# Cross-attention by head halves: another order of the steps on four engines

## What is computed

```
q = einsum('bld,hed->bhle', layernorm(x), Wq) + bq      # 8 heads of 128
k, v = the same from the context
scores = einsum over a window of 64 keys, spaced by (1,1,2,2,4,4,8,8)[head]
out = softmax(scores) @ v_win
x = x + out.reshape(..., 1024) @ Wc.T + bc
```

## Time and profile before

| | us |
|---|---|
| median of 3 runs | 492.98 (492.39 to 494.41) |
| the profiled execution | 493.77 |
| its span, first to last instruction | 491.9 |
| PE busy | 457.1 (93%) |
| DVE busy | 352.0 (72%) |
| ACT busy | 280.2 (57%) |
| POOL busy | 175.9 (36%) |
| DMA moved | 54.37 MB, mean 111 GB/s |

### The profile page before, as it was taken

How to read it: one execution, slowest core, us unless ns; L and a number is a source line. 1 busy time by engine, 2 the same in 40 slices (tenths; PEclk the granted TensorE clock), 3 DMA queues, 4 the chain that set the end, 5 groups by cost and what they waited for, 6 DMA issues and landing times.

```text
span 491.9 us, 11187 instructions
## 1 busy us (share of the span) xinstructions
PE 457.1 (93%) x3670; PEld 323.7 (66%) x3670; DVE 352.0 (72%) x837; ACT 280.2 (57%) x715; POOL 175.9 (36%) x184
## 2 busy tenths in 40 slices
PE   5999989999999999999999999989799999999960
PEld 2456469856458966556895646778676787888840
DVE  5754667796866778686678688898668885555476
ACT  4273756626547535555761665563666777877830
POOL 1230124040204313012504020234346877777541
PEclk9799999999999999999999999999999999999995
DMA  8901000034230031621003424608113247223655
GB/s 324 376 13 45 0 2 0 29 103 160 98 129 0 0 128 43 213 85 44 1 0 128 122 92 131 246 16 350 47 45 122 79 135 268 78 81 84 195 197 213
DMA packets 20410, 54.37 MB, mean 111 GB/s; under 512 B 3365, under 2 KB 9774, under 8 KB 19600
## 3 DMA queue, kind: packets, MB, share of 16 engines
q1 hardware_dynamic: 16336, 43.32, 24.7%
q0 software_dynamic: 3744, 9.47, 6.7%
q10 hardware_dynamic: 288, 1.05, 0.6%
HBM read 36.98 MB, written 17.76 MB: 111 GB/s over the span
## 4 chain that ended last, share of the span: by engine, by line
PE 45%; issue 25%; DVE 14%; POOL 8%; DMA 5%; DVEq 1%; POOLq 0%; ACT 0%; ACTq 0%; SPq 0%
PE pj L1469 16%; PE op L1702 7%; PE pj L1683 4%; DMA picked<-wch,dst_row 3%; PE sc L1658 2%; POOL pn L461 2%; POOL picked L490 2%; DMA cst<-rows,src_row 2%; PE pj L1795 2%; POOL rstd L430 1%; PE sc L1556 1%; DVE stats L769 1%; POOL cst L479 1%; PE ov L1469 1%; PE tpA L1805 1%
## 5 line engine op out<-in xcount | busy, mean ns | idle before, releaser
L1469 PE MATMUL pj<-up,up_f 128*128 128x512 f16 x480 | 109.6, 383 | 2.8 <-DVE down L1313 1.1
L1469 PEld LDWEIGHTS pj<-up,up_f 128*128 128x128 f16 x480 | 46.3, 99 | 59.5 <-DVE rope L939 4.6
L679 ACT ACTIVATE p<-sc,nm 128x128 f32<-128x128 f32 x128 | 45.4, 369 | 38.3 <-DVE nm L1308 38.1
L461 POOL TENSOR_TENSOR pn<-p,inv 128x256 f32<-128x256 f32 x64 | 37.9, 614 | 79.3 <-DVE inv L1261 79.3
L479 POOL DMA_INDIRECT cst<-rows,src_row x39 | 48.7, 1248 | 19.9 <-issue 7.6
L490 POOL DMA_INDIRECT picked<-wch,dst_row x39 | 41.5, 1064 | 26.4 <-DVE wch L1252 9.9
L430 POOL TENSOR_TENSOR rstd<-veps,nhalf 128x4 f32<-128x4 f32 (+1 forms) x13 | 12.7, 975 | 103.2 <-DVE veps L777 102.9
L551 ACT ACTIVATE down<-pj,bias 128x512 f32<-128x512 f32 x48 | 32.6, 686 | 26.5 <-PE pj L1469 26.3
L1469 PE MATMUL pj<-up_f,up 128*128 128x512 f16 x192 | 43.4, 379 | 0.0
L1702 PE MATMUL op<-wch,outs 128*128 128x256 f16 x240 | 40.2, 273 | 0.0
L1683 PE MATMUL pj<-pT,v 128*128 128x128 f32 x256 | 34.3, 279 | 1.3 <-DVE outs L1279 0.8
(11 more groups left out here) (265 smaller groups left out, 1025.5 us busy)
## 6 DMA issues: line engine op xcount, KB each, us to landing
raws<-in_staged SPq DMA_DIRECT2D x12, 512.0 KB, 5.4
split<-halved SPq DMA_DIRECT2D x12, 512.0 KB, 3.2
down<-split SPq DMA_DIRECT2D x4, 1024.0 KB, 8.6
rows<-row SPq DMA_DIRECT2D x4, 528.0 KB
small<-in_x SPq DMA_DIRECT2D x4, 512.0 KB, 3.6
up<-in_ctx SPq DMA_DIRECT2D x4, 512.0 KB, 4.8
v<-in_w SPq DMA_DIRECT2D x2, 1024.0 KB, 9.2
resid<-outs SPq DMA_DIRECT2D x4, 512.0 KB
```

The costliest lines, as they stand in the source:

```text
L461: pool.tensor_tensor(pn2[:, n % 2, k], p2[:, n % 2, k], inv2[:, n % 2, k].unsqueeze(2).to_broadcast([P, 2, P]), ALU.mult)\
L679: last = act.activation(p2[:, s, i, :], sc[s][:, i * P:(i + 1) * P], ACT.Exp, bias=nm2[:, s, i:i + 1], scale=1.0, accum_out=sum2[:, s, i:i ...
L1469: last = pe.matmul(out, w(c), v(c), start=(i == 0), stop=(i == len(terms) - 1))
```

## The change

The steps are ordered by half first: steps 0 to 3 are heads 0 to 3 of the four sequences, steps 4 to 7 heads 4 to 7. On every engine the distances are written anew: a transpose stands two steps behind the scores, a weighted sum three, an output product five. All queries are copied by ScalarE, and their last three projections stand in steps 0, 1 and 3. On VectorE `sums(n)` now follows reduction n in the same step, and the low half n - 4 stands ahead of reduction n. The output product is cut in two half products of 12 matmuls, `add_heads(m)`, for one step each; the sums of four sequences stay open in two banks (op and ov, in the fourth pass op and tpB), so `residual` runs in pairs at the end of the pass, and the next user of those banks waits for that. The transposes of the next tokens are two calls. ScalarE's `early(g + 1, 1)` moves from step 0 to step 5, its `part_high` from the end to step 6, VectorE's token low half from behind step 7 to step 6, its `part_low` from the end to step 7, and in the fourth pass `table` stands behind half product 4. The high and low halves of the outputs have four slots of four heads instead of two of eight. The number of matmuls, copies and exponentials is the same.

```diff
 # GpSimd, back
-                    if n >= 2 and n % 2 == 0:
-                        pool.wait_ge(tpA_full, TPA * g + 3 + (n - 2) // 2 + 1)
-                    if n >= 2 and n % 2 == 1:
-                        pool.wait_ge(blocks_turned, 4 * g + (n - 2) // 2 + 1)
+                    if 2 <= n < 6:
+                        pool.wait_ge(tpA_full, TPA * g + 3 + n - 1)
+                    if n >= 6:
+                        pool.wait_ge(blocks_turned, 4 * g + n - 5)
 # ScalarE, back (the old loop over 12 steps is taken out)
+                def outputs_high(m):
+                    if m >= 4:
+                        act.wait_ge(heads_added, 4 * g + m - 3)
+                    act.wait_ge(pj_full[m % 2], PJ * g + PROJ + m // 2 + 1)
+                    copy(oTh[:, m % 4].rearrange("p a b -> p (a b)"), pj[m % 2][:], MID).then_inc(o_hi, 1)
+
+                for n in range(8):
+                    s = n % 2
                     if n >= 4:
+                        outputs_high(n - 4)
...
                     last.then_inc(sc_free[s], 1)
-                    if more and n == 0:
+                    if n in (0, 1):
+                        project(g, 2, range(5 + n, 6 + n))
+                    if n == 3:
+                        project(g, 2, range(7, 8))
+                    if more and n == 5:
                         early(g + 1, 1)
+                    if more and n == 6:
+                        part_high(g, 0)
+                outputs_high(4)
+                outputs_high(5)
+                if more:
+                    early(g + 1, 0)
+                else:
+                    up_high()
+                outputs_high(6)
+                outputs_high(7)
...
 # VectorE, back
-                    dve.wait_ge(op_full, OP * g + 2 + b + 1)
+                    dve.wait_ge(op_full, OP * g + 2 + b // 2 * 2 + 2)
...
+                for n in range(8):
+                    s = n % 2
+                    if n >= 4:
                         outputs_low(n - 4)
...
+                    dve.wait_ge(sc_full[s], (SC[0] * g + 1, SC[1] * g)[s] + n // 2 + 1)
+                    dve.tensor_reduce(nm2[:, s, :], sc[s][:].rearrange("p (b t) -> p b t", b=4), AX, ALU.max,
+                                      negate=True).then_inc(neg2, 1)
+                    if n >= 2:
                         transposed(n - 2)
+                    if more and n == 6:
+                        early(g + 1, 3)
+                    sums(n)
+                    if more and n == 7:
                         part_low(g, 0)
...
                     if not more and n == 1:
                         old_counts()
...
+                transposed(6)
+                outputs_low(4)
+                transposed(7)
+                outputs_low(5)
+                if more:
+                    early(g + 1, 2)
+                    outputs_low(6)
+                    outputs_low(7)
+                    residual(0, op)
+                    residual(1, op)
+                    turned(g + 1)
+                    residual(2, ov)
+                    residual(3, ov)
+                else:
                     sources(TABLE_OLD, FULL, 0)
+                    outputs_low(6)
+                    residual(0, op)
                     residual(1, op)
+                    outputs_low(7)
                     tile_experts(full_first, full_n, FULL, 0)
                     dve.wait_ge(op_free, OP * g + 2 + 2)
                     norm(3, G - 1, x2, HALVES[0])
+                    residual(2, tpB)
+                    residual(3, tpB)
...
 # TensorE, front and back
                 for i, (bank_, full, free, use) in enumerate(first):
                     if r is not None:
                         pe.wait_ge(free, use)
+                        pe.wait_ge(op_free, OP * g)
...
+                    if n == 4:
+                        pe.wait_ge(pj_free[0], PJ * g + PROJ)
+                        pe.wait_ge(pj_free[1], PJ * g + PROJ)
...
+                for n in range(8):
+                    scores(n)
+                    if n in (0, 1):
+                        project(g, 2, range(5 + n, 6 + n))
+                    if n == 3:
+                        project(g, 2, range(7, 8))
+                    if n == 0 and not more:
+                        ranks(slice(0, OLD), 1, USE)
+                    if 2 <= n < 6:
                         turn_quad(n - 2)
+                    if n >= 3:
+                        weighted(n - 3)
+                    if n >= 5:
+                        add_heads(n - 5)
+                weighted(5)
+                add_heads(3)
+                weighted(6)
+                add_heads(4)
+                if more:
+                    turn_tokens_high(g + 1)
+                else:
+                    table(JO, FULL, 1, JO // 8, RANK_OLD)
+                weighted(7)
+                add_heads(5)
+                add_heads(6)
+                if more:
+                    turn_tokens_low(g + 1)
+                add_heads(7)
```

More of the change, by code:

```diff
@@ L166, in decoder @@
         room = Room(outs)
-        oTh, oTl = (room.cells(2 * H * P, F16).rearrange("p (s h t) -> p s h t", s=2, h=H) for _ in range(2))
+        oTh, oTl = (room.cells(2 * H * P, F16).rearrange("p (s h t) -> p s h t", s=4, h=4) for _ in range(2))
         x1, x2 = room.take(GB, D), room.take(GB, D)
@@ L1331, in back @@
-                    if more and n == 11:
-                        early(g + 1, 2)
-                    if more and n == 11:
-                        turned(g + 1)
                     if not more and n == 1:
@@ L1452, in _, with turn_part @@
         def _(pe):
-            def transposes(bankA, bankB, hi, lo, fullA, fullB, lows, n):
-                for dst, src, full in ((bankA, hi, fullA), (bankB, lo, fullB)):
-                    if full is fullB:
-                        pe.wait_ge(lows, n)
-                    view = dst[:].bitcast(F16)
-                    for c in range(KC):
-                        for b in range(GB):
-                            last = pe.transpose(view[:, c * TOK + b * P:c * TOK + (b + 1) * P],
-                                                src(b, c), identh[:])
-                    last.then_inc(full, 1)
+            def turn_part(bank_, src, full):
+                view = bank_[:].bitcast(F16)
+                for c in range(KC):
+                    for b in range(GB):
+                        last = pe.transpose(view[:, c * TOK + b * P:c * TOK + (b + 1) * P], src(b, c), identh[:])
+                last.then_inc(full, 1)
+            def transposes(bankA, bankB, hi, lo, fullA, fullB, lows, n):
+                turn_part(bankA, hi, fullA)
+                pe.wait_ge(lows, n)
+                turn_part(bankB, lo, fullB)
             def three(out, whi, wlo, xhi, xlo):
@@ L1638, in turn_quad @@
                             pe.wait_ge(norm2, 16 * g + 2 * m + i // 2 + 1)
[L1639 removed]
+                        last = pe.transpose(tpA[:, i * P:(i + 1) * P], pn2[:, m % 2, i, :], ident)
                     last.then_inc(tpA_full, 1)
                 def scores(n):
[L1644 removed]
+                    s, half, b = n % 2, n // 4, n % 4
                     t = slice(b * P, (b + 1) * P)
@@ new lines, in weighted @@
+                def weighted(m):
+                    k, use, half, b = m % 2, PROJ + m // 2 + 1, m // 4, m % 4
+                    if m < 4:
+                        pe.wait_ge(tpA_free, TPA * g + 3 + m + 1)
+                    else:
+                        pe.wait_ge(blocks_turned, 4 * g + m - 3)
+                    pe.wait_ge(pj_free[k], PJ * g + use - 1)
+                    for i in range(4):
+                        h = 4 * half + i
+                        last = pe.matmul(pj[k][:, i * P:(i + 1) * P], v2[:, b, h * DH:(h + 1) * DH],
+                                         pT2[:, m % 2, i, :], start=True, stop=True)
+                    last.then_inc(pj_full[k], 1)
@@ new lines, in add_heads @@
+                def add_heads(m):
+                    k, use, half, b = m % 2, PROJ + m // 2 + 1, m // 4, m % 4
+                    dst = op if b < 2 else ov if more else tpB
+                    if m == 0:
+                        pe.wait_ge(wc_lo, 1)
+                        pe.wait_ge(op_free, OP * g + 2)
+                    if m == 2 and more:
+                        pe.wait_ge(ov_free, OV * g + 2)
+                    pe.wait_ge(pj_free[k], PJ * g + use)
+                    for i in range(4):
+                        for j, (o, w) in enumerate(((oTh, wch), (oTl, wch), (oTh, wcl))):
+                            last = pe.matmul(dst[:, b % 2 * D:b % 2 * D + D], o[:, m % 4, i, :], w[:, 4 * half + i, :],
+                                             start=(m in (0, 2) and i == 0 and j == 0), stop=(half == 1 and i == 3 and j == 2),
+                                             skip_group_check=True)
+                    last.then_inc(heads_added if half == 0 else op_full, 1)
@@ L1714, in _ @@
             pe.wait_ge(ready, 1)
-            turn_tokens(0, after=False)
```

(4 more changed lines are left out.)

157 lines of the change are left out of this document (28 added, 129 removed).

## The result

The changed kernel takes **512.27 us** (median of 4 runs, 510.19 to 513.83); the kernel before, on the same chip, 492.69. The ratio is 1.0398, 95% interval [1.0374, 1.0422]: **slower**, as forecast, by 19.6 us where 16.0 had been worked out. The profiled execution took 512.64 us, its span is 510.7 [before: 493.77 and 491.9].

A forecast was written before the change was run, and what follows sets the result against it. TensorE was taken as busy nearly all of a pass, so only waits could change; passes losing 3.1 + 3.3 + 2.8 + 6.8 = 16.0 us gave 509.0 us predicted, range 500 to 516.

The forecast's parts named there:

- What bounds: waits, not work: TensorE in a pass: 39.5 us of work in 41.3, the same matmuls in the new order, so only waits can change.
- The inverse ahead of the next reduction: VectorE, in order, waits for exponentials n before inverse n, so reduction n+1 waits too: softmax becomes a closed two-engine loop.
- The first turn: Softmax loop's first steps: reduction, exponentials, inverse and two hand-overs between VectorE and ScalarE, 2.35 us per turn.
- a turn with outputs: Loop from step 4 on: exponentials, ScalarE's high half, VectorE's low half, reduction and hand-overs, 3.38 us.
- with a long copy in it: Loop turns from 5 to 6 and 6 to 7, with a 0.95 us ScalarE copy added: 4.33 us.
- The long copies inside the loop: ScalarE's token and weight-part copies, 0.95 us each, lengthen late turns to 4.33, slower than TensorE's 3.31 of work.
- the prediction's rival: ScalarE's two long copies find room outside the loop; passes stay 41.4 us, only the fourth loses: 500 us; chance 0.10.
- The query copies on ScalarE: Copies 5 to 7 take 0.69 us each; query 7's, behind exponentials 3, makes TensorE wait 1.3 us before scores 4.
- The passes: First, second and third attention pass, up to the front's first projection: 3.1, 3.3 and 2.8 us longer.
- Fourth pass: VectorE builds expert tables behind each inverse, no longer under the exponentials: its end 6.9 us later, expert stage 6.8.
- less four reductions, three inverses, ... the tables of steps 1 to 4 take 6.05: Fourth pass, VectorE: old 11.15 us from reduction 1 to 5, minus other work, leaves 6.05 us of table instructions.
- The clock: Rival: TensorE's 3.1 us wait for query 7 in the fourth pass drops its clock, 2.8 us more: 512; chance 0.06.

The follow-up runs named there:

- run 5: Changed kernel with late inverse, VectorE query copies, moved token and weight-part copies in passes 1 to 3, tables first in pass 4: 488.69 us, ratio 0.9935.
- run 1: Changed kernel with the inverse of step n-1 put behind the reduction of step n again, in all passes: 500.9 us, ratio 1.0162.
- run 4: Changed kernel with the fourth pass's tables, and elsewhere the weight part's low half, ahead of the inverse on VectorE: 501.56 us, ratio 1.019.
- run 2: Changed kernel with ScalarE's token copy back behind exponentials 0 and both weight-part halves back at the pass's end: 506.53 us, ratio 1.0314.
- run 3: Changed kernel with query copies 5, 6 and 7 given back to VectorE, behind reductions 0, 1 and 3: 509.67 us, ratio 1.0356.
- run 7: Changed kernel with unread matmuls in TensorE's two long waits, ahead of the fourth pass's scores 4 and behind that pass: 510.23 us, ratio 1.0365.

## Why the prediction was right, and where its size was off

*What bounds: waits, not work.* Right. TensorE's work per pass was put at 39.5 us from the earlier trace rows; the second pass of run 5 is at 39.9 without a wait.

*The inverse ahead of the next reduction.* Right, and the largest single part: run 1 takes 11.4 us away, and run 4, which keeps the loop and fills it, 10.7. The first turn was put at 2.35 us, and 2.36 was measured in the second pass; a turn with outputs at 3.38, measured 3.36 (from 4 to 5); with a long copy in it at 4.33, measured 4.29 twice. In the second pass reductions 4 to 7 were worked out at 11.1, 14.4, 18.8 and 23.1 us after reduction 0, and stand at 11.3, 14.7, 19.0 and 23.2. But the prediction put all these turns under the inverse, and only those up to reduction 3 are its doing in the first three passes: run 1 leaves the later ones as they are. Its own sum for the turn with outputs has no inverse in it; what closes that turn is the low half ahead of the reduction. No run moves the low half back, so the cost of that place by itself is not shown.

*The parts of a pass.* In the second pass run 1 gives back 1.97 us, run 2 2.35 and run 3 0.77, together 5.1; run 5, which undoes all three, gives back 4.9 of 44.81. So in these passes the long copies weigh no less than the inverse. The inverse is the chief cause in the fourth pass, where the tables stand behind it (6.9 in run 1).

*The long copies inside the loop.* Right: the prediction's rival said that without them the pass would be "41.4, as now"; run 2 has 42.5, so the rival was 1.1 too good (the wait for exponentials 1 was 0.88 where it had 0.4, and TensorE's work 39.9 where it had 39.5).

*The query copies on ScalarE.* The waits of 1.3 (measured 1.37) and the 0.69 us per copy (measured mean 688 ns in 60 copies) were right. What the wait is worth was not separated: 0.8 us a pass (run 3). The Trainium skill, "ScalarE: Activation LUTs", "Rules for kernel authors", gives additions and multiplications, of which these copies consist, to VectorE. For speed the trace does not agree (0.69 on ScalarE, 0.75 on VectorE); for this kernel the advice was right all the same, by place: on ScalarE the copy stands behind the exponentials.

*The passes.* 3.3, 3.3 and 2.9 forecast by the timeline's starts, 3.5, 3.5 and 3.2 measured.

*Fourth pass.* Here a term was mis-sized: **6.8 us forecast, 9.15 measured** at the first expert tile, 8.45 at VectorE's end. The step that failed is "less four reductions, three inverses, ... the tables of steps 1 to 4 take 6.05": it carried the tables' times over from a place where the normalization overlapped them less. Behind the inverse they run right beside the normalization that this inverse releases. Reduction 0 to 7 took 29.31 us instead of the 27.85 worked out, 1.46 more; the six instructions of run 4 account for 1.5. That is the whole of VectorE's excess (8.45 against 6.9). Of the last 0.7, between VectorE's end and the first expert tile, 0.33 is order: the last rows' low half comes 8.78 us later after the pass's start (55.08 against 46.30, VectorE's L798 and L791), but before the change one residual (L1297 at 345.51) still stood between it and VectorE's end, and now that stands earlier. The prediction took VectorE's end for the rows. The other 0.37 lies behind the rows, where TensorE ran at the lower clock; run 7 got 0.18 of it back, and the rest stays open.

*The clock.* The rival's condition came true: 3.66 us of wait for query 7 (3.1 forecast), and a granted clock of 0.66 over the 10 us that hold it. Its price did not: with the full clock in run 7 the reductions come no sooner, so the half-clock matmuls were not on the chain.

*Front and free edits.* Fronts of 39.2, 39.2 and 39.4, as before; nothing of the two output banks, the earlier write or the later loads shows. *Start and runs:* the profiled span is 18.8 longer (the six stages give 19.6, and the passes began 0.8 sooner), the medians differ by 19.6.

## What to carry to other kernels

A small instruction can close a loop between two in-order engines (here 0.18 us of inverse, put in front of the next reduction instead of behind it), and then each step costs the round trip: look for what is queued behind its wait, and either let it lag one step or put work that is due anyway between the two. Opening one loop can leave a second one that sets the same pace (here the one over the outputs), so look again at which wait ends last. The new order was worth having (0.65%), but only once these costs were undone; before a reordering is judged as a whole, take it apart. And a long copy that was free in a wait costs its full length once it stands inside a loop.

## What the runs showed of the hardware

VectorE and GpSimd slow each other for certain instructions only. Beside a normalization on GpSimd, VectorE's instructions with two inputs in SBUF (L1094, L1107, L1051) and some short one-input ones (L1105, L1141, L1143) ended 0.02 to 0.22 us behind the end of one of its halves and took 0.19 to 0.46 us more each than in run 4, and a 1024-column instruction that came first (L1080) put 0.83 us on GpSimd's pair. The reductions, transposed copies and low halves that read PSUM kept their 0.65 to 0.69 us throughout. The Trainium skill has the rule, "SBUF — State Buffer", "Who interferes with whom": the two engines share one pair of ports, which is held for a whole instruction, and only VectorE instructions with two SBUF inputs, or copies, casts and scalar operations in a two-port mode, need it. The traces of after and of run 4 agree, in the order too: L1141 began 0.04 us behind a half and waited for it, L1080 began 0.23 us ahead of one and kept its 1.20. I had read the same lengths in the trace of before (0.53 for an 8-column instruction) without asking why.

Over the 10 us that hold a wait of TensorE of 3.66 us the mean granted clock was 0.66, and 0.70 over those that hold one of 4.99 us; behind the second wait, from 363.6 to 368 us, it was 0.50, the lower of the two levels. With matmuls in the waits it was 1.00 both times. In this kernel that was worth nothing that could be measured in the total.
